# Masking, summing and averaging the attention scores: four wide passes, or passes of one tile and one head

## The reference, cut to what matters

```python
def _L1_xattn_ref(x_text, x_vision, text_mask, vision_mask, Wq, Wk, Wv, ...):
    ...
    scores = jnp.einsum('bthd,bghd->bhtg', Q, K) / np.sqrt(DH).astype(np.float32)
    scores = jnp.where(vision_mask[:, None, None, :], scores, -jnp.inf)
    topv, topi = jax.lax.top_k(scores, K_TOP)
    probs = jax.nn.softmax(topv, axis=-1)
    ...
    attn = jnp.zeros_like(scores).at[bi, hi, ti, topi].set(probs)
    attn_mean = attn.mean(axis=1)
    V = x_vision @ Wv
    c_t = jnp.einsum('btg,bgd->btd', attn_mean, V)
    c_t = c_t * text_mask[..., None]
    x = layernorm(x_text, g_norm_in, b_norm_in)
    scale_in, shift_in = jnp.split(c_t @ W_film_in + b_film_in, 2, axis=-1)
    ...
```

## Time and profile before

| | |
|---|---|
| median of 3 runs | 1811.51 us (1810.51 to 1813.48) |
| the profiled execution's own time | 1824.46 us |
| its span in the trace | 1822.8 us |
| PE busy | 1610.8 us (88%), 8584 instructions |
| DVE busy | 1278.0 us (70%), 4255 instructions |
| ACT busy | 909.9 us (50%) |
| POOL busy | 649.1 us (36%) |
| mean granted clock of TensorE | 0.938 |

### The profile page before, as it was taken

One profiled execution on the slowest core, in us unless ns is written; L12 is line 12 of the kernel. 1 busy time (PEld: TensorE's weight loads), 2 busy tenths in 40 slices (PEclk: granted clock), 3 DMA queues, 4 the chain that ended last, 5 costly groups with the idle time before them and its releaser, 6 DMA issues.

```text
span 1822.8 us, 27958 instructions
## 1 busy us (share of the span) xinstructions
PE 1610.8 (88%) x8584; PEld 1330.1 (73%) x8584; DVE 1278.0 (70%) x4255; ACT 909.9 (50%) x1943; POOL 649.1 (36%) x1005
## 2 busy tenths in 40 slices
PE   6899999997599999978869999999999999998774
PEld 3677778776489999874647777777877777786553
DVE  3566777766247666224478899999999999987751
ACT  2454444442142222226656766667776667763221
POOL 1022322222101000015435556666655655552111
PEclk9899999999699999998879999999999999999877
DMA  9992000000796565545200000000000000000000
GB/s 258 289 290 75 15 16 13 12 13 24 256 309 199 153 202 162 174 139 212 73 7 8 13 20 19 20 13 7 20 19 20 20 13 7 8 14 13 7 6 12
DMA packets 145477, 143.47 MB, mean 79 GB/s; under 512 B 22587, under 2 KB 128525, under 8 KB 145074
## 3 DMA queue, kind: packets, MB, share of 16 engines
q1 hardware_dynamic: 128321, 119.78, 21.4%
q10 hardware_dynamic: 13936, 13.50, 2.3%
q0 software_dynamic: 3072, 8.39, 1.5%
HBM read 87.71 MB, written 53.94 MB: 78 GB/s over the span
## 4 chain that ended last, share of the span: by engine, by line
PE 28%; DVE 21%; issue 3%; ACT 2%; POOL 1%; DMA 0%; POOLq 0%; DVEq 0%; ACTq 0%
PE E_pK L2346 6%; PE E_pK L2305 3%; PE E_pS L2413 3%; DVE E_wk L1850 3%; PE E_pY L2462 3%; DVE E_ex L1782 2%; DVE E_m L1843 2%; PE E_pY L2293 2%; PE E_pU L2422 2%; PE E_pY L2431 2%; DVE E_st L1715 1%; PE E_pY L2305 1%; PE E_pT L2287 1%; PE E_pY L2356 1%; PE E_pU L2452 1%
## 5 line engine op out<-in xcount | busy, mean ns | idle before, releaser
L1294 ACT ACTIVATE F_uT<-F_puT,F_b 128x128 f32<-128x128 f32 x312 | 88.4, 371 | 214.6 <-PE F_puT L1351 165.4
L1351 PEld LDWEIGHTS F_puT<-F_hT,F_W 128*128 128x128 f32 x1248 | 157.8, 207 | 10.3 <-DVE F_hT L1089 8.1
L1351 PE MATMUL F_puT<-F_hT,F_W 128*128 128x128 f32 x1248 | 159.6, 291 | 5.7 <-DVE F_hT L1089 5.7
L1599 POOL TENSOR_SCALAR E_var<-E_mv 128x2 f32<-128x2 f32 x80 | 44.6, 558 | 309.8 <-DVE E_mv L1719 308.2
L1364 PE MATMUL F_py<-C_W,F_uT 128*128 x624 | 141.2, 379 | 0.6 <-DVE C_shared L1101 0.6
L2452 PE MATMUL E_pU<-E_xT,E_W 128*128 128x256 f32 x512 | 122.5, 395 | 5.3 <-ACT E_hid L2193 3.1
L1364 PEld LDWEIGHTS F_py<-C_W,F_uT 128*128 128x128 f32 x624 | 115.5, 190 | 15.1 <-issue 1.0
L2356 PE MATMUL E_pY<-E_Wcv,E_hid 128*128 128x256 f32 x512 | 118.3, 385 | 8.6 <-issue 8.2
L2462 PE MATMUL E_pY<-E_W,E_hid 128*128 128x256 f32 x512 | 119.1, 387 | 0.1
L2452 PEld LDWEIGHTS E_pU<-E_xT,E_W 128*128 128x128 f32 x512 | 101.6, 199 | 21.7 <-ACT E_hid L2193 3.9
L2346 PE MATMUL E_pK<-E_cmix,E_Wck 128*128 128x256 f32 x512 | 115.9, 381 | 0.0
(11 more groups left out here) (432 smaller groups left out, 4133.4 us busy)
## 6 DMA issues: line engine op xcount, KB each, us to landing
F_W<-in_L_ffn_W SPq DMA_DIRECT2D x39, 1024.0 KB, 6.0
sorted_x<-zero SPq DMA_DIRECT2D x8, 4096.0 KB, 31.6
C_W<-in_L_ffn_W ACTq DMA_DIRECT2D x8, 1024.0 KB, 7.6
F_xs<-sorted_x SPq DMA_DIRECT2D x39, 128.0 KB, 2.7
F_b<-in_L_ffn_b SPq DMA_DIRECT2D x39, 128.0 KB, 3.2
sorted_y<-C_shared ACTq DMA_DIRECT2D x39, 128.0 KB, 2.9
context_film<-E_W SPq DMA_DIRECT2D x8, 512.0 KB
out<-E_tB SPq DMA_DIRECT2D x16, 256.0 KB, 2.2
```

The costliest lines, as they stand in the source:

```text
L1294: last = nc.scalar.activation(uT[:, i % 2, f, :], p_uT[:, i % 2, half, (f % 4) * P:(f % 4 + 1) * P], ACT.Gelu, bias=b1[:, i % 2, f:f + 1])
L1351: last = nc.tensor.matmul(p_uT[:, i % 2, half, (f % 4) * P:(f % 4 + 1) * P], W1[:, i % WB, kb, f * P:(f + 1) * P], hT[:, i % 2, kb, :], st ...
```

## The change

`average` computes the same with other passes. The product with the mask is done for one tile and one head at a time (8 instructions of 77 elements), each of which also writes the sum of what it produced into its column of `sm`, so the sum over all 616 elements is gone. The two small instructions on the sums stay. The product with the scale and the sum over the heads are replaced: the first head of each tile is multiplied by its scale into `am` (2 instructions of 77), then each further head is multiplied by its scale and added to `am` (3 heads x 2 tiles, 6 instructions of 77). Each of these waits for the instruction before last, which wrote the same half of `am`. The last one raises the semaphore for TensorE.

```diff
             def average(j):
                 settled()
                 dve.wait_ge(e["ex"], j + 1)
-                chained(v.scalar_tensor_tensor(out=ex[:], in0=wk[:], scalar=TAKEN, in1=ex[:], op0=ALU.is_equal, op1=ALU.mult))
-                settled()
-                chained(v.tensor_reduce(sm[:], ex[:], AX.X, ALU.add))
+                for t in range(2):
+                    for hd in range(H):
+                        last = v.scalar_tensor_tensor(out=ex[:, t, hd, :], in0=wk[:, t, hd, :], scalar=TAKEN, in1=ex[:, t, hd, :],
+                                                      op0=ALU.is_equal, op1=ALU.mult, accum_out=sm[:, t, hd:hd + 1])
+                chained(last)
                 settled()
                 chained(v.reciprocal(rs[:], sm[:]))
                 settled()
                 chained(v.tensor_tensor(rs[:], rs[:], tm[:, 2 * j:2 * j + 2].unsqueeze(2).to_broadcast([P, 2, H]), ALU.mult))
                 settled()
-                chained(v.tensor_tensor(ex[:], ex[:], rs[:].unsqueeze(3).to_broadcast([P, 2, H, J]), ALU.mult))
-                settled()
                 past(dve, e["amp"], j - 1)
-                v.tensor_reduce(am[:], ex[:].rearrange("p t h j -> p t j h"), AX.X, ALU.add).then_inc(e["am"], 1)
+                for t in range(2):
+                    chained(v.tensor_scalar(am[:, t, :], ex[:, t, 0, :], rs[:, t, 0:1], None, ALU.mult))
+                for hd in range(1, H):
+                    for t in range(2):
+                        dve.wait_ge(step["dve"], steps - 1)
+                        last = v.scalar_tensor_tensor(out=am[:, t, :], in0=ex[:, t, hd, :], scalar=rs[:, t, hd:hd + 1],
+                                                      in1=am[:, t, :], op0=ALU.mult, op1=ALU.add)
+                        if hd < H - 1 or t == 0:
+                            chained(last)
+                last.then_inc(e["am"], 1)
```

## The result

The changed kernel takes 1804.27 us as the median of 11 runs (1797.71 to 1809.69) against 1813.66 us for the kernel before (11 runs, 1809.58 to 1831.79). The two medians are 9.4 us apart; the ratio is 0.9939, 95% interval 0.9915 to 0.9963, so 11 us less with an interval of 7 to 15. Run once more on another occasion (e11), it came to 0.9954 (0.9933 to 0.9975), 8.3 us less. The prediction was 1803.1 us, 8.4 us less.

What follows compares the result with a forecast made beforehand. The prediction took a loop through TensorE and VectorE's `average` to bound the turn. Gains of 0.26 and 0.34 us make 0.60 a turn, 8.4 us over 14 turns: 1811.5 to 1803.1 us, own range 1801 to 1806, full range 1799.5 to 1812.5.

Steps and rivals of the forecast that it cites:

- What bounds the kernel: A loop through TensorE and VectorE sets the 53.6 us turn; each 0.1 us of `average` moves it as much.
- Masking and sums: In `average`, seven passes at 0.16 us plus 0.28 make 1.40 us for 1.66: 0.26 us gained each turn.
- half-rate rival: Accumulating masking passes with both sources in SBUF take 0.24 us each; 0.6 us slower, 1812.1 us, no change; chance 0.11.
- draining rival: In `average`, masking pass and accumulator read each wait for the one before; 6.2 us slower, 1817.7 us; chance 0.10.
- Scale and mean: In `average`, two multiplications at 0.17 us, five multiply-adds at 0.21, plus 0.29: 1.68 us for 2.02, 0.34 gained.
- The distance of 0.21 us read off L1926: Start-to-start price of a 77-element multiply-add with a column as scalar, from a 256-element instruction at 0.39 us.
- Waits on the pass before last: Among the six multiply-adds: a pass finishes 0.29 us after its start, its waiter comes 0.42 after, so no stall.
- 0.60 us a turn: Gain of both parts of `average` together, 0.26 plus 0.34 us, leaving 0.87 of TensorE's 1.47 us wait.
- The end of the gain at 1.47 us: At TensorE's transpose of the average: gains up to its 1.47 us wait pass whole; beyond, another path holds the turn.
- the path that was named: The path by the norm TensorE waits 0.98 us for at L2287, and TensorE's queue; holds the turn beyond 1.47 us.
- 14 batches at 0.60: Gain of 0.60 us in 14 turns, none in the last two batches, where TensorE does not wait: 8.4 us.

Runs made afterwards that it cites:

- e11: Changed kernel run once more, unchanged, on another occasion; turn 53.03 us, time ratio 0.9954 to the kernel before.
- e1: Kernel before with only the masking part: eight accumulating passes replace the wide masking pass and sum; turn 53.36 us for 53.61, time ratio 1.0031 to the kernel before.
- e2: Kernel before with only the second part: two multiplications and six multiply-adds for scale and sum over heads; turn 53.28 us for 53.61, ratio 0.9966.
- e6: Changed kernel with masking passes not writing sums, the wide sum back as its own instruction; turn 53.77 us for 53.03, ratio 0.9974 to the kernel before.
- e7: Changed kernel with a constant 0.25 replacing the column of inverse sums in all eight second-part passes; turn 52.55 us for 53.03, ratio 0.9883 to the kernel before.
- e8: Changed kernel with one tile's multiply-adds after the other's, each waiting for the one just before; turn 53.63 us for 53.03, ratio 0.9994 to the kernel before.
- the two repeats: Changed kernel run again unchanged (turn 53.03 us, ratio 0.9954 to the kernel before), and masking part alone run again (turn 53.36 us, ratio 0.9998).
- e3: Changed kernel with TensorE's transpose of the average after three quarters of the products, not half; turn 52.15 us for 53.03, ratio 0.9894 to the kernel before.
- e4: Kernel before with TensorE's transpose of the average after three quarters of the products, not half; turn 52.77 us for 53.61, ratio 0.9896.
- e5: Changed kernel without its six multiply-adds, only the first head entering the mean; turn 51.91 us for 53.03, ratio 0.9819 to the kernel before.

## Why the prediction was right

- *What bounds the kernel.* Right. The turn follows the average one for one in the changed kernel, e1, e2, e6, e7, e8 and the two repeats, in both directions (to 0.03 us), and TensorE's work moved into the wait gives as much again (e3, e4).
- *Masking and sums, 1.40 us for 1.66.* Measured 1.40. The half-rate rival and the draining rival both fall by the passes' distance of 0.16 and their overlap (each lasts 0.23 to 0.24 us). The Trainium skill's remark in the Vector Engine (DVE) Microarchitecture Reference, section "Points that are easy to get wrong", that a scalar_tensor_tensor with two SBUF sources that are not bf16 runs at half rate, is not borne out here with an accumulator either: 0.16 us a pass, where half rate would be 0.24. Of the section "The DRAIN you can't avoid" the prediction tells only half: the Trainium skill, VectorE: DVE Perf Modes, says in the same paragraph that a next operation that is not held starts earlier, and these passes, 0.16 us apart and 0.23 long, agree.
- *Scale and mean, 1.68 us for 2.02.* Measured 0.34 less (1.74 for 2.08 with the way to TensorE). The distance of 0.21 us read off L1926 was right, and e7 shows 0.06 of it to be the column's.
- *Waits on the pass before last cost nothing.* Right, and e8 shows what they would have cost: 0.13 us each.
- *0.60 us a turn.* Measured 0.58; the wait left is 0.88 for 0.87.
- *The end of the gain at 1.47 us.* Not reached by the change; e5 puts it at 1.70 us, 0.23 further than the wait shown, and held by the path that was named.
- *14 batches at 0.60, so 8.4 us.* From the first average's transpose to the last one's are 7.6 us less (804.43 to 796.83), with 0.4 less ahead of it in the stage and 0.9 behind. The 7.6 are 11 steady turns with 6.3, the second turn with 0.6 (54.71 for 55.28), and a first, 14th and 15th turn that moved by +3.15, -3.08 and -0.8. The first is longer with TensorE's clock (0.87 granted for 0.93). The 14th has the higher clock (0.93 for 0.91) and also a wait for VectorE's `E_cmix` of 0.59 us in place of 2.27; the 15th is shorter at a lower clock (0.79 for 0.83). Why these two moved is open. The sum counted 14 equal gains, of which the traces show 12 in turns; that the rest came out right, since the ends cancel, is luck. For the mask part alone they do not cancel, and there a sum of this kind was wrong by the whole 3.5 us.
- *What I left out.* That the whole time of one kernel moves by 25 us with the granted clock (1805.09 to 1830.10), 15 us of it between two traces in stages that the change does not touch, which makes a single span useless for a change of this size.

## What to carry to other kernels

Find the loop that sets the length of a turn, and price a change by the distance between starts on it, not by busy time: here 20 more instructions in each batch made the engine's path shorter. A sum taken along in a pass costs almost nothing (0.01 us), a wide pass cut up costs 0.07 us for each extra piece (1.28 us for 0.80 in eight), and dependent small passes should alternate between two results. When a queue waits in the middle of a block of independent work, move the wait to where just enough of it is left to cover the next copy: one changed constant gave more (0.84 to 0.88 us a turn) than the change studied here.

## What the runs showed of the hardware that I had not expected

- TensorE's granted clock after the wait of some 11 us for the first average is 0.50, the lower level, for about 8 us in some kernels and 15 to 16 in others, which makes the first turn 55.7 or 58.6 to 59.1 us. It was the same in both profiled executions of each of two kernels. Which of the two a kernel gets is not settled: the kernels with the early return (before, e6, e8) had waited 11.35 to 11.50 us, those with the late one 10.29 to 11.37. e5, which had waited 9.51, lies between, with 13 to 14 us and a first turn of 56.49.
- The time of one kernel follows the mean granted clock: 1805.09 us at 0.949, 1830.10 at 0.937.
- The idle time shown behind a block of 24 products is 0.16 us less than the delay of the next start: they are shown as 5.34 us long, and in e5 the transpose behind them starts after 5.18.
